# Second attention of a fused transformer kernel: the softmax product moves from VectorE to GpSimd, in two parts, in an unrolled GpSimd program

## What is computed

```
x = x + attention(layernorm(x), ctx)          # the stage that changes
q, k, v = x @ Wq, ctx @ Wk, ctx @ Wv          # 8 heads of 64
sim  = einsum(q, k) * 64 ** -0.5              # 128 x 77 for each head
attn = softmax(sim, axis=-1)
out  = (attn @ v) @ Wo + bo
```

## Time and profile before

| | |
|---|---|
| median of three runs | 2375.3 us (2373.95 to 2376.54) |
| the profiled execution's own time | 2378.55 us |
| its span in the profile | 2376.7 us, 49088 instructions |
| TensorE busy | 2222.7 us (94%) |
| VectorE busy | 1830.1 us (77%) |
| ScalarE busy | 1443.7 us (61%) |
| GpSimd busy | 741.3 us (31%) |
| second attention | about 766 to 1087 us of the span |

### The profile page before, as it was taken

How to read it: one execution, slowest core, us unless ns; L and a number is a source line. 1 busy time by engine, 2 the same in 40 slices (tenths; PEclk the granted TensorE clock), 3 DMA queues, 4 the chain that set the end, 5 groups by cost and what they waited for, 6 DMA issues and landing times.

```text
span 2376.7 us, 49088 instructions
## 1 busy us (share of the span) xinstructions
PE 2222.7 (94%) x14668; PEld 1903.4 (80%) x14669; DVE 1830.1 (77%) x4454; ACT 1443.7 (61%) x3010; POOL 741.3 (31%) x1022
## 2 busy tenths in 40 slices
PE   7899999999899999996389999999997999979998
PEld 6788888888698888873177888888886888879998
DVE  3798888898966788887857788787887666865666
ACT  5566666665444677766475666666664564636666
POOL 2255546555412122226130111111112342422334
PEclk9999999999899999996599999999998999979999
DMA  8444544445200454540044544544541000125445
GB/s 219 119 142 126 147 142 138 137 133 152 67 11 15 135 140 129 138 118 16 1 123 121 148 130 134 154 140 142 146 120 52 1 1 4 36 58 140 140 141 160
DMA packets 461646, 256.58 MB, mean 108 GB/s; under 512 B 25664, under 2 KB 442332, under 8 KB 461532
## 3 DMA queue, kind: packets, MB, share of 16 engines
q1 hardware_dynamic: 461532, 255.27, 38.3%
HBM read 150.10 MB, written 105.12 MB: 107 GB/s over the span
## 4 chain that ended last, share of the span: by engine, by line
PE 79%; DVE 11%; ACT 5%; issue 3%; POOL 1%; DVEq 0%; ACTq 0%; POOLq 0%
PE ps_o L1023 13%; PE ps_s L1010 12%; PE ps_t L995 7%; PE ps_p L89 6%; PE ps_p L91 6%; PE ps_p L90 6%; PE ps_o L1706 3%; PE ps_t L1706 3%; PE ps_t L3371 2%; PE ps_s L3353 2%; PE ps_o L3371 2%; PE ps_s L89 2%; PE ps_s L90 2%; PE ps_s L91 2%; DVE a_sm L1353 2%
## 5 line engine op out<-in xcount | busy, mean ns | idle before, releaser
L1023 PEld LDWEIGHTS ps_o<-a_val,a_pt 128*128 128x128 f32 (+2 forms) x3200 | 416.0, 193 | 39.9 <-issue 9.5
L1023 PE MATMUL ps_o<-a_val,a_pt 128*128 128x128 f32 (+2 forms) x3200 | 428.5, 277 | 5.7 <-ACT a_pt L1207 3.9
L1010 PE MATMUL ps_s<-a_keys,a_zt 128*128 128x308 f32 (+1 forms) x1024 | 415.1, 492 | 5.6 <-DVE a_e L1345 3.4
L1353 DVE TENSOR_REDUCE a_sm<-a_e 128x16 f32<-128x1232 f32 (+1 forms) x192 | 234.2, 1220 | 183.4 <-ACT a_e L1215 183.1
L1177 ACT ACTIVATE a_stage<-ps_p 128x512 f32<-128x512 f32 (+1 forms) x349 | 208.7, 598 | 251.7 <-PE ps_p L91 249.3
L1207 ACT ACTIVATE a_pt<-ps_t 128x512 f32<-128x512 f32 (+1 forms) x448 | 225.1, 505 | 144.5 <-PE ps_t L995 143.2
L995 PE MATMUL ps_t<-ident,a_e 128*128 128x128 f32 (+1 forms) x1600 | 263.3, 277 | 28.6 <-POOL a_e L1370 14.0
L1168 ACT ACTIVATE a_keys<-ps_p 128x308 f32<-128x308 f32 x566 | 241.2, 427 | 73.3 <-PE ps_p L91 73.3
L89 PE MATMUL ps_p<-ct_hi,a_mt_hi 96*128 (+1 forms) x566 | 275.0, 486 | 0.0
L1215 ACT ACTIVATE a_e<-a_e 128x1232 f32<-128x1232 f32 (+1 forms) x192 | 204.0, 1063 | 70.4 <-DVE a_e L1345 54.4
L1370 POOL TENSOR_TENSOR a_e<-a_e,a_rs 128x539 f32<-128x539 f32 (+1 forms) x192 | 165.9, 892 | 229.0 <-DVE a_rs L1358 227.7
(11 more groups left out here) (436 smaller groups left out, 4995.4 us busy)
## 6 DMA issues: line engine op xcount, KB each, us to landing
a_vals<-a_stage SPq DMA_DIRECT2D x160, 512.0 KB, 3.5
a_val<-a_vals SPq DMA_DIRECT2D x128, 576.0 KB
f_w<-in_L_ffn_W_dram SPq DMA_DIRECT2D x129, 256.0 KB, 2.7
a_vals<-a_stage SPq DMA_DIRECT2D x40, 416.0 KB
a_val<-a_vals SPq DMA_DIRECT2D x64, 256.0 KB
a_val<-a_vals SPq DMA_DIRECT2D x128, 40.0 KB
x<-in_x_dram SPq DMA_DIRECT2D x8, 512.0 KB, 7.1
out_dram<-x SPq DMA_DIRECT2D x7, 512.0 KB, 6.7
```

The costliest lines, as they stand in the source:

```text
L1010: mm = eng.matmul(o, self.zt[:, par, cols], self.keys[:, par, k, h0:h0 + nh, :], start=True, stop=True)
L1023: mm = eng.matmul(c.ps_o[:, (i % 2) * P:(i % 2 + 1) * P], self.pt[0:r, n, :], self.val[0:r, i % 2, n, :], start=(n == 0), stop=(n == self. ...
L1353: eng.tensor_reduce(self.sm[:, :], e, AX.X, ALU.add).then_inc(st.sem, 1)
```

## The change

The product of the exponentials with the reciprocal sums leaves normalise() on VectorE for phases with 8 heads too, and GpSimd does it in weigh(), as it does for the masked phase. With 616 columns, weigh makes two parts: heads 0 to 6 (539 columns) and head 7 (77). TensorE waits for part one before the first four chunks and for part two before the fifth. GpSimd's program for the phase is the one written out for 64 tiles, in this order for tile t = 4g + k: the product of tile t+1; then at k = 1 the bias of group g+1, at k = 2 root(g-1), at k = 3 of odd groups the window copy. The first and the third attention stay as they were.

```diff
+        self.weighed = self.masked or heads == 8
...
-        self.prob_parts = self.uses if self.masked else 1
+        self.prob_parts = self.uses if self.weighed else 1
...
         if self.masked:
             eng.tensor_scalar(self.rs[:, par, :], self.rs[:, par, :], self.some_key[:, 1:2], None, ALU.mult)\
                .then_inc(st.sem, 1)
+        if self.weighed:
             return
         eng.tensor_tensor(e, e, bc(self.rs[:, par, :], KEYS), ALU.mult).then_inc(self.probs_ready.sem, 1)
 
-    def weigh_masked(self, eng, t, par):
+    def weigh(self, eng, t, par):
...
-        if self.masked:
+        if self.weighed:
             self.ln.pool(eng, 1)
...
-        if self.masked:
-            self.gpsimd_masked(eng, v_last)
+        if self.weighed:
+            self.gpsimd_weighed(eng, v_last)
             return
...
-    def gpsimd_masked(self, eng, v_last):
-
-        self.weigh_masked(eng, 0, 0)
+    def gpsimd_weighed(self, eng, v_last):
+
+        self.weigh(eng, 0, 0)
         for t in range(BATCH):
             g, k = t // GT, t % GT
             if t + 1 < BATCH:
-                self.weigh_masked(eng, t + 1, (k + 1) % 2)
+                self.weigh(eng, t + 1, (k + 1) % 2)
             if k == 1 and g + 1 < GROUPS:
                 self.ln.pool_bias(eng, g + 1)
             elif k == 2 and g >= 1:
-                self.next_stats.pool(eng, g - 1)
+                if self.left:
+                    self.left.root(eng, g - 1)
+                else:
+                    self.next_stats.pool(eng, g - 1)
             elif k == 3:
                 w = t // self.WIN
                 if g % 2 == 1 and w + 2 < self.WINDOWS:
...
-        self.next_stats.pool(eng, GROUPS - 1)
+        if self.left:
+            self.left.root(eng, GROUPS - 1)
+        else:
+            self.next_stats.pool(eng, GROUPS - 1)
```

## The result

The changed kernel takes 2419.7 us (2417.39 to 2422.44, four runs) against 2374.62 us before on the same chip: 1.0183 times the time, 95% interval 1.0167 to 1.0200, slower by some 45 us. The forecast was 2420, slower. The profiled execution took 2422.44 us, its span is 2420.6 against 2376.7. The whole of it lies in the second attention: from the first transposes of probabilities to the end of the last weighted sum it took 297.2 us before (788.85 to 1086.06) and takes 342.9 now (788.72 to 1131.61), and what stands ahead of and behind it differs by less than 2 us.

The account below looks back on a forecast made before the run. TensorE was taken to bound the second attention (258.25 of 260 us busy). 19.2 + 15.7 + 2.4 - 3 - 3 = +31 us, with +14 for the clock +45, on the median of 2375.3 gives 2420 us; range 2397 to 2440.

Parts of the forecast that it names:

- The stalls: Borders between groups: TensorE idles while GpSimd's product waits behind root; 19.2 us at six mid-window, 15.7 at seven between windows.
- the end's sum: Second attention from t=57 on, product off VectorE, less the border at t=60: net 3 us gained (0 to 5).
- The window copy: At six borders between windows GpSimd's copy follows the product and delays a projection some 0.4 us each: 2.4 us.
- The product's 0.3 us: Part one takes 1.09 us on GpSimd instead of 0.80; the 0.3 us is lost only in a window's eighth tile.
- What comes back: Gains from relieving VectorE in the second attention: 3 us in the stride (0 to 8.7), 3 at the end (0 to 5).
- The clock: TensorE's clock falls after the new gaps at nine of thirteen full borders, 1.5 us each: +14 us (0 to 24).
- The sum: All terms in the second attention: +31 us without the clock, +45 with it.
- this mark: Sign in the timeline of the second attention: the period of two groups grows by 5 to 7 us.
- Case 2: Same stalls at the borders, TensorE's clock kept: 2406 us (2396 to 2412); chance 0.22.
- case 3: Clock falls at every border, in places for twice as long: 2430 up to 2454 us; chance 0.13.
- case 4: Squares land early enough that waiting for them costs TensorE nothing, and relieved VectorE wins: 2368 us; chance 0.06.
- case 5: Nothing to measure (within 0.2%, 4.8 us): border stalls of some 0.6 us that the gains cancel; chance 0.04.

Follow-up runs that it names:

- the earlier copy: Against the kernel with root one group later: window copy moved to the third tile of odd groups, root to the fourth tile; 0.9964 of the time before.

## Why the prediction was right

- **The stalls** were the step that decided, and each part of their price held: release, root, part one and TensorE's release came to 2.84 us in mid window, and to 2.83 to 2.97 over all 14 borders. Six mid-window borders: 3.02 us idle against 3.2 (18.1 us in all against 19.2). Seven between windows: 2.34 to 2.57 against 2.24 (17.0 against 15.7). The one at t=60: 2.17, forecast 1.5 and inside the end's sum.
- **The window copy** was put at 0.4 us at six borders. In the changed kernel TensorE waits for it once, 0.4 us, behind the border at t=40, the one of the six where the clock had stayed up; at the others the low clock makes TensorE late for it. In the kernels with the clock up it is 0.5 us, six times, but worth less than that, as the earlier copy showed. The term was up to 2.4 us too large.
- **The product's 0.3 us** on TensorE shows only in the eighth tile (0.37), seven times, as said, and in the last tiles; never as a loss in each tile.
- **What comes back.** With root one group later a window is 0.3 us shorter than before, 2.0 us over six; in the changed kernel, with stalls and clock taken off, 0.4 us, some 2.7 over seven, against 3. The end: from t=56 to t=63 TensorE took 29.3 us (1099.49 to 1128.82), before 31.0 (1052.26 to 1083.27). That is 1.7 us less with two falls of the clock in it, which the next item counts; without their 3.4 us the end gave back some 5 where I had 3.
- **The clock** was the largest unknown. I had said nine falls at 1.5 us, 14 us. There were 11, with 38 us of low clock: some 18 us of work. Filling the stalls gave 13.5 to 15 back. By the profile's own low stretches this term was some 4 us small. My reason for where the clock falls was not borne out: it fell at six of the seven shorter gaps and at four of the six longer ones.
- **The sum** over a window: the borders are 45.2 us apart on average (828.37 to 1099.49, six windows) and were 37.7. Of the 7.5 us, 5.4 are stalls, about 2.6 the clock, and 0.4 go back. I had written that the period would grow by 5 to 7, so this mark was too low by the clock's share. The total of +45 against 45.7 us in the stage was nearer than its terms, and that much is luck: the clock cost 4 us more than forecast, the window copy 2 less, and the end gave back 2 more. The one term without which there is no loss, the stalls, was right by itself (35.2 us at the thirteen full borders, 34.9 forecast).
- **A bound.** Case 2's lower end of 2396 doesn't follow from its own bounds: 2375.3 + 37.3 less 13.7 is 2399. Nothing hung on it.
- **The rivals.** The clock at every border (case 3) was not so here, but came with 1.1 us more stall. The unchanged clock (case 2) came with 1.6 us less. That the squares land early enough (case 4) did not happen; it can be had by calling root a tile or a group later. Stalls small enough to cancel the gains (case 5) did not happen either: TensorE had nothing else to do at the borders.

## What to carry to other kernels

When work moves to an idle engine, read that engine's queue rather than its busy share: the first thing to ask is which wait comes to stand in front of the moved work, and when what it waits for is produced. Here a root that nobody wanted for a long time stood ahead of a product wanted at once; moved behind it, the same change gained 0.1 to 0.4% (3 to 6 us in the stage) instead of losing 1.8%. A stall of a microsecond or two on TensorE is to be priced together with the clock that it may cost.

## What the runs showed of the hardware

- The clock's answer to a gap has much chance in it. At the fourteen borders there was no fall with gaps of 0.6 to 1.4 us (root's operations behind the product), 11 falls with 2.2 to 3.0 us (the changed kernel), 14 with 3.2 to 4.1 (root's last operation twice), five of these for twice as long. So 1.1 us more of stall at each border cost 2 us. The first tile's gap of 2.15 us was followed by a fall with root one group later, and by none in the changed kernel.
- Matmuls without use, run in the gap, held the clock up and made the kernel faster.
- Before the change, VectorE's two-input product took 0.80 us when GpSimd was idle and up to 1.17 us beside GpSimd's bias and root. VectorE's operations that stay in the stage ran almost as before beside GpSimd's product (the shift 469 ns for 466, the sum 792 for 790).
- The same product of 616 elements took 1.22 us on GpSimd as one instruction and 1.40 as two (1.09 and 0.31), against 0.80 on VectorE.
